# A four-layer graph network on one core: where and how often GpSimd clears a small tile between its gathers

## Time and profile before

| | us |
|---|---|
| median of 3 runs | 2548.76 |
| lowest, highest | 2537.23, 2555.19 |
| profiled execution | 2554.49 |
| its span, first to last instruction | 2552.7 |
| POOL busy | 1719.4 (67%) |
| PE busy | 1578.3 (62%) |
| DVE busy | 1075.0 (42%) |
| ACT busy | 486.5 (19%) |

### The profile page before, as it was taken

The page is one execution under the profiler, slowest core; times in us unless marked ns, Lnnn a source line. Parts: engine busy times, 40 slices in busy tenths (PEclk is TensorE's granted clock), DMA queues, the critical chain, the costliest instruction groups (busy, mean ns, idle before and its releaser), DMA issues.

```text
span 2552.7 us, 27909 instructions
## 1 busy us (share of the span) xinstructions
PE 1578.3 (62%) x8443; PEld 1386.8 (54%) x8443; DVE 1075.0 (42%) x2213; ACT 486.5 (19%) x1153; POOL 1719.4 (67%) x1653
## 2 busy tenths in 40 slices
PE   5664333233568878777777777778676644646664
PEld 2343323233467777776677777767534434535564
DVE  5573101010646666545222222222537643344487
ACT  3200000000166667521100000000212111110020
POOL 5487777777467777771777777776157777767720
PEclk8765555555577887767555555555658755556677
DMA  6432121322111111111222222222162322222210
GB/s 209 167 89 88 24 88 23 72 43 44 25 29 38 34 39 34 34 26 42 54 61 53 61 54 56 58 54 51 41 226 78 74 67 60 65 57 65 60 41 13
DMA packets 159862, 159.26 MB, mean 62 GB/s; under 512 B 108361, under 2 KB 111993, under 8 KB 158748
## 3 DMA queue, kind: packets, MB, share of 16 engines
q0 software_dynamic: 48352, 68.42, 12.2%
q1 hardware_dynamic: 111372, 89.07, 12.0%
HBM read 118.71 MB, written 46.06 MB: 65 GB/s over the span
## 4 chain that ended last, share of the span: by engine, by line
POOL 38%; DVE 17%; issue 17%; another core or an unknown queue 14%; PE 9%; DMA 2%; ACT 1%; DVEq 1%; SPq 1%; ACTq 0%; POOLq 0%
POOL flat L591 33%; DVE flat L838 7%; POOL quiet L579 6%; DVE oh L1057 2%; DVE oh L799 2%; PE ps L1402 2%; PE ps L1355 2%; DVE msg L1048 1%; DMA table<-flat 1%; PE ps L1380 1%; PE ps L1590 1%; PE ps L1367 1%; PE ps L1655 1%; PE ps L1330 1%
## 5 line engine op out<-in xcount | busy, mean ns | idle before, releaser
L591 POOL DMA_INDIRECT flat<-table,flat x1061 | 1113.0, 1049 | 463.7 <-issue 300.2
L1402 PE MATMUL ps<-flat,oh 128*128 x1664 | 331.3, 381 | 418.6 <-DMA flat<-table,flat 307.1
L1402 PEld LDWEIGHTS ps<-flat,oh 128*128 128x128 f32 x1664 | 315.1, 291 | 445.7 <-issue 443.3
L799 DVE TENSOR_TENSOR oh<-iota_n,drel 128x1024 f32<-128x1024 f32 x156 | 190.5, 1223 | 702.1 <-PE ps L1402 247.5
L591 POOL DMA_INDIRECT flat<-table,tile_idx x359 | 346.3, 965 | 125.5 <-issue 99.6
L1367 PE MATMUL ps<-msg,oh 128*128 128x64 f32 x832 | 190.5, 424 | 133.6 <-issue 67.4
L1367 PEld LDWEIGHTS ps<-msg,oh 128*128 128x128 f32 x832 | 181.4, 331 | 142.4 <-issue 142.4
L1380 PE MATMUL ps<-uvT,flat 128*128 128x192 bf16 x2200 | 221.4, 271 | 16.6 <-ACT flat L1205 16.3
L1380 PEld LDWEIGHTS ps<-uvT,flat 128*128 128x128 bf16 x2200 | 215.7, 110 | 21.9 <-issue 17.7
L579 POOL MEMSET quiet<- 128x1400 bf16 x144 | 187.4, 1301 | 30.8 <-DVE base L1051 30.8
L1525 PEld LDWEIGHTS ps<-uvT,ohT 128*128 128x128 f32 x832 | 191.9, 316 | 19.6 <-issue 1.9
(11 more groups left out here) (321 smaller groups left out, 1471.3 us busy)
## 6 DMA issues: line engine op xcount, KB each, us to landing
table<-flat SPq DMA_DIRECT2D x52, 512.0 KB
drow<-slot_node SPq DMA_DIRECT2D x104, 256.0 KB
flat<-table,flat POOLq DMA_INDIRECT x1061
flat<-edge_attr_by_slot SPq DMA_DIRECT2D x52, 128.0 KB
edge_attr_padded<-edge_attr SPq DMA_DIRECT2D x1, 6250.0 KB
flat<-table,tile_idx POOLq DMA_INDIRECT x359
flat<-tile_source SPq DMA_DIRECT2D x22, 256.0 KB
edge_attr_by_slot<-flat SPq DMA_DIRECT2D x2, 2048.0 KB
```

Of the source, the lines that this page charges most:

```text
L591: nc.gpsimd.indirect_dma_start(dest(t % PLACES), None, table, at_).then_inc(tile_gat[k % TRING], 16)
L799: V.tensor_tensor(oh[:, b], iota_n[:].unsqueeze(1).broadcast_to([P, SG, P]), drel[:, g * SG:(g + 1) * SG].unsqueeze(2).broadcast_to([P, SG ...
L1402: last = T.matmul(acc[:, bass.ds(n[j] * pitch + shift, width)], oh[:, b % 2, j, :], got[:, bass.ds(place[j], width)], start=False, stop=Tr ...
```

## The change

In the first layer the clear stands only ahead of groups 4, 8, ..., 48 (12 times, not 48), and there ahead of the ring's wait. In the third and fourth layer it stays at every group but changes places with the ring's wait.

```diff
             for g in range(TG):
+                if g and g % 4 == 0:
+                    breath()
                 if g >= TRING:
                     pool.wait_ge(s("used"), g - TRING + 3 + 3)
-                if g:
-                    breath()
                 gather_tiles(0, g, table0_d...)
...
             for g in range(TG):
+                if g:
+                    breath()
                 if g >= TRING:
                     pool.wait_ge(s("edge_sum"), g - TRING + 3 + 2)
-                if g:
-                    breath()
                 gather_tiles(2, g, table2_d...)
...
+                if k:
+                    breath()
                 if k >= TRING:
                     pool.wait_ge(s("scored"), k - TRING + 3 + 3)
                     pool.wait_ge(s("values"), k - TRING + 3 + 1)
-                if k:
-                    breath()
                 gather_tiles(3, k, table3_d...)
```

## The result

The changed kernel takes 2567.88 us (median of 20 runs), the kernel before 2556.95 beside it (20 runs): a ratio of 1.0037, with an interval of 1.0020 to 1.0055. Forecast were 2504 us and 45 saved; it lost about 9 by the ratio, 10.9 by the medians. The profiled execution took 2562.93 us, with a span of 2560.8.

What follows compares the result with a forecast made beforehand. The prediction took GpSimd's own issue to pace the first layer. 45 us for 36 clears and 0 for the changed order, off the 2548.8 us median, gave 2504 us, range 2486 to 2522.

Steps and rivals of the forecast that it cites:

- The bound: First layer: paced by GpSimd's own issue, clear and gathers in one line, 11.29 us from clear to clear.
- 36 clears fewer, 45 us: First layer: each removed clear saves 1.26 us, together 45; a group without one takes 10.03 us.
- this is all on the path if nothing else becomes late: First layer: the whole 45 us shortens the run, provided sums, landing, ring and gather lengths hold.
- the wait stays at nothing by some 5 us: First layer, group 8: GpSimd begins at about 157 us, after group 3's sums end at 152.4, so no ring wait.
- the ring's wait in the first layer: First layer: GpSimd held until a group's sums free its ring place; its appearance would show the forecast wrong.
- Collisions: First layer: one-hots lengthening gathers; grid unmoved from group 12 on, 7 us to either side for the first twelve groups.
- Clear ahead of the wait: Swapping clear and ring's wait: 0 in first and third layer; attention, six holds, 0 with 12 us to either side.
- Rival B: First layer: clears keep TensorE's issue going; without them 12.5 against 11.3 us a group, 2593; slower 0.06, no change (2553) 0.05.
- 41 us is less than the 68 after which it appeared: Against Rival B: first-layer gather runs grow to 41 us; second-layer sums came in pieces after 68 us of unbroken gathers.
- The attention has the gaps with a clear at every group: Against Rival B: in the attention products come in pieces despite a clear at every group, so clears do not prevent it.
- 6.3 us of slack in each group: Against Rival B: in the first layer TensorE still idles 6.3 us a group, sums taking 3.67 of 10.03.
- The range: Whole kernel: 2486 to 2522 us, from bounds of 7 for collisions, 12 for the attention, some 9 for the median.

Runs made afterwards that it cites:

- N: Jobs in which the kernel before takes 2407 to 2410 us and no wait in the list says "remote" (no late signal).
- L: Jobs in which the kernel before takes 2551 to 2602 us and TensorE's signals come late; the prediction's profile and the result are of this kind.
- every fourth: Kernel before with the first layer's clear only at every fourth group, order unchanged: 2363.59 us in N, 2575.59 against 2558.33 in L.
- none: Kernel before with no clear in the first layer, the rest unchanged: 2346.86 us in N, 2568.41 us in L.
- tiny: Kernel before with the first layer's clear of 8 columns in place of 1400, at every group: 2358.68 us in N, 2565.00 us in L.

## Why the prediction was wrong

*The bound.* Right in N, where GpSimd's issue is nearly the whole chain. In L the chain had 14% for "another core or an unknown queue", and the forecast read past them. On a program of one core that row is a finding.

*36 clears fewer, 45 us.* The size was right: 45.6 us in N, and undisturbed groups 10.0 us apart in L. That N gave the number does not save the forecast for L, where it was made. The step that failed is "this is all on the path if nothing else becomes late, which I go through in turn": the turn took in sums, landings, ring and collisions, each as work of a known length, and not the time from TensorE's last product to the waiter. In L that time grew to 41 us and more, and the ring took back 49.1 us in six holds, where the forecast had "the wait stays at nothing by some 5 us". That sentence is about group 8, and group 8 has the largest hold: GpSimd was there at 159.1 (forecast: about 157), but the sums of group 3 ended at 186.05 (forecast: 152.4, taken over from the trace before), since ScalarE had waited 55.87 us for a product of TensorE's, and GpSimd stood for 27.73 us. The forecast named the ring's wait in the first layer as a sign that it is wrong, and that is the sign that came.

*Collisions.* Right where nothing is late: with a whole clear gone the grid doesn't move (951 to 960 ns a gather in N), with half a clear gone it does (1012 ns). In L, where late one-hots fall anywhere on the grid, the changed kernel's gathers took 1005 ns on the mean, before 959, and 7.2 us more over the layer. The Trainium skill's rule (SBUF — State Buffer, "Who interferes with whom") was borne out for VectorE against GpSimd. The conclusion drawn from it, that the removed clears protect nothing, was wrong in L: they protect a signal, on which that section says nothing, and no run here shows an SBUF conflict of TensorE.

*Clear ahead of the wait.* First and third layer: right, 0 (the third layer takes 699.9 us to the attention's first gather, 699.0 before). Attention: the forecast took 0 with 12 to either side. Measured alone: -2 us in L, with an interval that includes 0, and 0 in N. Five gathers wait, at 3.3 to 3.9 us, not six.

*Rival B* was the nearest and had 0.11, of which 0.06 for the slower side. Its mechanism was half right: runs of gathers without a break do it, but as signals that come late, most of them after GpSimd has stopped, more than as sums in pieces, so its sum by group lengths (12.5 against 11.3) doesn't apply. The three reasons against it fail one by one. "41 us is less than the 68 after which it appeared": runs of 32 gathers were enough, and so were runs of 8 with 0.97 us between. "The attention has the gaps with a clear at every group": it does, but in the first layer a pause of 1.56 us at every group does prevent them. "6.3 us of slack in each group" counts for nothing against one stall of 32 us.

*The range* held neither case it should have weighed: in N the kernel before is itself at 2408. In ratio the forecast was 0.982; N gave 0.9826.

**What stays open.** What makes a job L or N; which path TensorE's signals share with GpSimd's gathers; why in the third layer and the attention they are late in spite of a clear at every group; why some arrive without a pause; what L's 177 us consist of, nearly all of them outside the first layer's gathers; and whether the total or the spacing of pauses counts. That in L the layer takes 540 to 556 us with any clears from none to full says that pauses and stalls trade evenly there, but not why.

## What to carry to other kernels

In these traces of a program of one core, a one-hot whose wait ends "remote" always started 1.5 us or more after the work it waited for; in step it is 0.04. Some late ones are put down to "issue" or to TensorE, so the label alone doesn't find them all: before removing a filler instruction, compare the end of the work with the start of its waiter, and ask whether the filler is the pause in which signals get through. Idle that looks like slack per group doesn't cover a stall that is longer than a group. And a gain that depends on the job's condition has to be measured in both: leaving out all clears is worth 7.4% in N (in L it was not measured), and leaving out two thirds of them costs 1.4% in L.

## What the runs showed of the hardware

- Two conditions of the same kernel, 2407 to 2410 and 2551 to 2602 us. The length of an undisturbed gather (0.94 us), of a group of sums (3.67) and the landing (about 1.8) are the same in both; in the second, TensorE's completion signals, and at times its own issue, are late.
- In L, under gathers 0.30 us apart, one-hots of the first layer started up to 44.9 us after the sums that they needed (no clear in the first and third layer), and a copy of ScalarE's 46.8 us after its product (changed kernel). The latest came once the ring had stopped GpSimd, 2.6 to 8.5 us after (change, every fourth, none, tiny); others, up to 36.5 us late (tiny clear), came while its gathers went on. In the first layer a pause of 1.56 or 2.2 us at every group kept the one-hots in step, 0.40 did not, 0.97 did in part; in the third layer 1.56 did not.
- TensorE's waits for landed rows and for VectorE's one-hots showed no such lateness in the same stretches.
